# First expert stage: down products from high and low parts, down weights kept in SBUF, up weights of each tile fetched from DRAM

## The reference, cut to what matters

```python
xhat = (x - mu) * rsqrt(var + LN_EPS)
xn = xhat * ln_g[e] + ln_b[e]                      # 256 features
h = relu(xn @ w1[e].T + b1[e])                     # up: 256 -> 1024
y = x + h @ w2[e].T + b2[e]                        # down: 1024 -> 256
out = a * y + (1 - a) * x                          # a = sigmoid(x @ centroids[e])
```

## Time and profile before

| | us |
|---|---|
| median of 3 runs | 1677.14 (1675.1 to 1678.51) |
| profiled execution, device time | 1680.14 |
| its span in the trace | 1678.3 |
| PE busy in the span | 1491.0 (89%) |
| DVE busy | 1002.0 (60%) |
| ACT busy | 882.1 (53%) |
| POOL busy | 833.9 (50%) |
| last step of `routing` 0 on DVE ends | 562.6 |
| up(0) starts on PE | 572.8 |
| finish(31) on DVE ends | 813.2 |

### The profile page before, as it was taken

The page is one execution under the profiler, slowest core; times in us unless marked ns, Lnnn a source line. Parts: engine busy times, 40 slices in busy tenths (PEclk is TensorE's granted clock), DMA queues, the critical chain, the costliest instruction groups (busy, mean ns, idle before and its releaser), DMA issues. The chain is left out here.

```text
span 1678.3 us, 50328 instructions
## 1 busy us (share of the span) xinstructions
PE 1491.0 (89%) x17142; PEld 1239.3 (74%) x17143; DVE 1002.0 (60%) x2228; ACT 882.1 (53%) x1626; POOL 833.9 (50%) x1145
## 2 busy tenths in 40 slices
PE   6999999999996499999599999999999646999677
PEld 4777777777774499999478888888888524888566
DVE  3677677677663433333247677777777577777544
ACT  3777777777774244443266566656665323333233
POOL 3576676666663111111256666666666305333263
PEclk8999999999996699999799999999999757999889
DMA  5111211110100611111212222221110042333475
GB/s 145 58 53 58 83 59 48 59 34 23 34 18 12 261 35 38 38 34 34 86 33 75 67 92 71 75 90 44 44 48 25 16 141 88 129 130 131 127 232 182
DMA packets 63184, 127.98 MB, mean 76 GB/s; under 512 B 11106, under 2 KB 35870, under 8 KB 59590
## 3 DMA queue, kind: packets, MB, share of 16 engines
q1 hardware_dynamic: 52798, 99.03, 18.2%
q0 software_dynamic: 10320, 28.07, 6.0%
HBM read 94.77 MB, written 32.29 MB: 76 GB/s over the span
## 5 line engine op out<-in xcount | busy, mean ns | idle before, releaser
L1017 DVE TENSOR_REDUCE a_mx<-a_SM 100x2 bf16<-100x722 f32 x384 | 351.4, 915 | 201.1 <-PE a_SM L459 197.8
L737 ACT ACTIVATE a_Pr<-a_ST 120x1600 f32<-120x1600 f32 (+3 forms) x192 | 225.0, 1172 | 125.5 <-PE a_ST L491 123.8
L501 PE MATMUL a_M<-a_Pr,a_V 120*32 120x100 f32 (+3 forms) x4608 | 176.2, 257 | 0.0
L459 PE MATMUL a_SM<-a_KT,a_QM 32*100 32x362 f32 x768 | 152.6, 393 | 25.9 <-DVE a_mx L1017 25.6
L787 POOL TENSOR_TENSOR a_rstd<-a_ve,a_powers 100x1 f32<-100x1 f32 x192 | 118.7, 618 | 96.2 <-DVE a_ve L986 94.5
L501 PEld LDWEIGHTS a_M<-a_Pr,a_V 120*32 120x32 f32 (+3 forms) x4608 | 135.8, 120 | 21.7 <-issue 12.8
L862 POOL TENSOR_TENSOR a_cl<-a_ct,a_ch 128x724 fp32r<-128x724 f32 x62 | 107.3, 1731 | 42.9 <-DVE a_o L1059 42.9
L386 PE MATMUL a_M<-a_wvh,a_ch 128*120 128x256 f32 (+1 forms) x384 | 123.8, 322 | 3.1 <-ACT a_KF L623 3.1
L852 POOL TENSOR_TENSOR a_KL<-a_KF,a_KT 128x724 fp32r<-128x724 f32 x64 | 111.5, 1742 | 26.7 <-ACT a_KT L631 15.4
L1534 PEld LDWEIGHTS e_PH<-e_xT,e_wS 128*128 128x128 f32 x1024 | 120.9, 194 | 4.2 <-issue 2.7
L1534 PE MATMUL e_PH<-e_xT,e_wS 128*128 128x128 f32 x1024 | 121.4, 277 | 2.1 <-DVE e_xT L1612 2.1
(11 more groups left out here) (219 smaller groups left out, 3872.3 us busy)
## 6 DMA issues: line engine op xcount, KB each, us to landing
w<-in_E_w SPq DMA_DIRECT2D x24, 1024.0 KB, 7.1
a_ct<-in_ctx SPq DMA_DIRECT2D x64, 362.0 KB, 3.2
gated_rows<-g_hs SPq DMA_DIRECT2D x57, 256.0 KB
keep_rows<-a_keep SPq DMA_DIRECT2D x64, 100.0 KB
tile_rows<-e_y SPq DMA_DIRECT2D x32, 128.0 KB, 1.7
X<-in_E_b SPq DMA_DIRECT2D x1, 4096.0 KB
x_rows<-X SPq DMA_DIRECT2D x32, 100.0 KB
g_xr<-x_rows SPq DMA_DIRECT2D x25, 128.0 KB
```

What stands on the lines that cost most here:

```text
L459: last = nc.tensor.matmul(SM[0:LQ, half, 0:LKP], QM[b.p][rows, chunk, m, :], KT[b.p][rows, chunk, :], start=True, stop=True)
L501: last = nc.tensor.matmul(M0[VW * j:VW * (j + 1), g * LQ:(g + 1) * LQ], V[b.p][0:n, kt, h, :], Pr[0:n, kt, POS[h] * LQ:(POS[h] + 1) * LQ], ...
L737: nc.scalar.activation(Pr[0:n, s, :].rearrange("p (r q) -> p r q", r=GROUPS), ST[0:n, :, 0:PER * LQ], ACT.Exp, scale=SCALE).then_inc(exp_d ...
L1017: V_.tensor_reduce(pair, SM[0:LQ, :, 0:LK], AX_X, ALU.max).then_inc(max_done, 1)
```

## The change

1. The buffer `w1`, which attention 0 fills, now gets the down weights of the first expert layer. The second buffer and its 8 MB of transfers in `routing` 0 are gone.
2. The up weights of each tile come straight from DRAM into `wS`: SP reads the tile's expert and starts a transfer of 1 MB (`up_weights`). It waits for `h_ps` as ACT's copy did. ACT's copy is gone. SP's order is up_weights(j+3), store(j).
3. The down product is made from parts: a value is split into a high part, rounded to fp32r, and a low part, the rest. Per tile ACT makes the high part of `hT` (128x1024) and of the tile's down weights (128x2048); DVE subtracts for the low part of the weights (128x2048) and of the second half of `hT` (128x512); POOL subtracts for the first half of `hT` (128x512). PE does 24 fp32r products (high by high, high by low, low by high) in place of 8 fp32 products, and waits for all three low parts.
4. DVE's order becomes columns(j+2), hidden(j+1), hidden_low(j+1), down_low(j+1), finish(j).
5. `xs` has two buffers, `gather` starts two tiles ahead and takes its row numbers straight from `toks`, without the copy. POOL's stream is written out for all 32 tiles and holds gather(j+2), hidden_low(j).

```diff
@@ expert_tiles: buffers @@
-        w1 = env["w1"]
+        w2 = env["w1"][:].rearrange("p e c f -> p e (c f)")
         ident = env["kept"]["ident"]
-        w2 = env["second_buf"]
         lng, lnb, b1, b2 = (dst for dst, _ in env["small"])
         small_loaded, SMALL = env["small_loaded"], 16 * len(env["small"])
-        gidx = sb("gidx", [128, 1], I32)
-        xs = sb("xs", [128, D])
+        xs = [sb(f"xs{p}", [128, D]) for p in range(2)]
         xT = sb("xT", [128, DC, 128])
-        hT = [sb(f"hT{p}", [128, G, 128]) for p in range(2)]
+        hT_at = [(nc.sbuf_base + 31) // 32 * 32]
+        hT = [sb("hT0", [128, G, 128])]
+        hT_at.append((nc.sbuf_base + 31) // 32 * 32)
+        hT.append(sb("hT1", [128, G, 128]))
+        hT_low = [nc.alloc_sbuf_tensor_at(f"{tag}hT_low{p}", [128, G, 128], F32R, offset=hT_at[p]) for p in range(2)]
+        hT_high = [sb(f"hT_high{p}", [128, G, 128], F32R) for p in range(2)]
+        w2_high = [sb(f"w2_high{p}", [128, G, D], F32R) for p in range(2)]
+        w2_low = [sb(f"w2_low{p}", [128, G, D], F32R) for p in range(2)]
         wS = [sb(f"wS{p}", [128, DC, F]) for p in range(2)]
         y = [sb(f"y{p}", [128, D]) for p in range(2)]
...
         @block.sync
         def _(sp):
-            def store(j, p, r):
+            def up_weights(j, p, first):
+                e = expert_of(sp, j)
+                if not first:
+                    sp.wait_ge(h_ps, j * 2 - 2)
+                sp.dma_start(wS[p][:].rearrange("p c f -> p (c f)"),
+                             t["w1"][:, bass.ds(e, 1)].rearrange("p o c f -> p (o c f)")).then_inc(w_staged[p], 16)
+            def store(j, p):
                 sp.wait_ge(y_ready, j + 1)
                 sp.dma_start(t["ys"][bass.ds(j * 128, 128), :], y[p][:]).then_inc(y_stored[p], 16)
-            with sp.Fori(0, NT // 2) as i:
+            up_weights(0, 0, True)
+            up_weights(1, 1, True)
+            up_weights(2, 0, False)
+            with sp.Fori(0, NT // 2 - 2) as i:
                 for p in range(2):
-                    store(i * 2 + p, p, i)
-            if NT % 2:
-                store(NT - 1, 0, NT // 2)
-            sp.wait_ge(y_stored[0], 16 * ((NT + 1) // 2))
-            sp.wait_ge(y_stored[1], 16 * (NT // 2))
+                    up_weights(i * 2 + (p + 3), 1 - p, False)
+                    store(i * 2 + p, p)
+            for j in range(NT // 2 * 2 - 4, NT):
+                if j + 3 < NT:
+                    up_weights(j + 3, (j + 3) % 2, False)
+                store(j, j % 2)
+            for p in range(2):
+                sp.wait_ge(y_stored[p], 16 * (NT // 2))
         @block.gpsimd
         def _(pool):
-            def gather(j, first):
-                if not first:
-                    pool.wait_ge(x_ps, j)
-                pool.sem_inc(turns, 1)
-                nc.gpsimd.tensor_copy(gidx[:], env["toks"][:, bass.ds(j, 1)]).then_inc(idx_ready, 1)
-                pool.wait_ge(idx_ready, j + 1)
-                pool.sem_inc(turns, 1)
-                nc.gpsimd.indirect_dma_start(xs[:], None, t["keep"], bass.IndirectOffsetOnAxis(gidx[:], 0)
-                                             ).then_inc(rows_loaded, 16)
-            gather(0, True)
-            with pool.Fori(1, NT) as j:
-                gather(j, False)
-        def expert_of(engine, j):
-            return engine.value_load(env["tile_e"][0:1, bass.ds(j, 1)], min_val=0, max_val=E - 1)
+            def gather(j):
+                if j >= 2:
+                    pool.wait_ge(x_ps, j - 1)
+                nc.gpsimd.indirect_dma_start(xs[j % 2][:], None, t["keep"],
+                                             bass.IndirectOffsetOnAxis(env["toks"][:, j:j + 1], 0)
+                                             ).then_inc(rows_loaded[j % 2], 16)
+            def hidden_low(j):
+                p = j % 2
+                pool.wait_ge(h_high, j + 1)
+                nc.gpsimd.tensor_tensor(hT_low[p][:, 0:HALF].rearrange("p g q -> p (g q)"),
+                                        hT[p][:, 0:HALF].rearrange("p g q -> p (g q)"),
+                                        hT_high[p][:, 0:HALF].rearrange("p g q -> p (g q)"), ALU.subtract
+                                        ).then_inc(h_low_pool, 1)
+            gather(0)
+            gather(1)
+            for j in range(NT):
+                if j + 2 < NT:
+                    gather(j + 2)
+                hidden_low(j)
         @block.tensor
         def _(pe):
-            def rows(j, first):
-                pe.wait_ge(rows_loaded, j * 16 + 16)
+            def rows(j, p, r, first):
+                pe.wait_ge(rows_loaded[p], r * 16 + 16)
                 if not first:
                     pe.wait_ge(xT_ready, j)
                 for c in range(DC):
-                    last = nc.tensor.transpose(PX[:, c * 128:(c + 1) * 128], xs[:, c * 128:(c + 1) * 128], ident[:])
+                    last = nc.tensor.transpose(PX[:, c * 128:(c + 1) * 128], xs[p][:, c * 128:(c + 1) * 128], ident[:])
                 last.then_inc(x_ps, 1)
...
             def down(j, p, far):
-                e = expert_of(pe, j)
-                pe.wait_ge(hT_act, j + 1)
-                pe.wait_ge(hT_dve, j + 1)
+                pe.wait_ge(h_low_dve, j + 1)
+                pe.wait_ge(h_low_pool, j + 1)
+                pe.wait_ge(w2_low_ready, j + 1)
                 if far >= 2:
                     pe.wait_ge(y_ready, j - 1)
-                for g in range(G):
-                    rhs = w2[:, bass.ds(e, 1), g, :].rearrange("p o f -> p (o f)")
-                    last = nc.tensor.matmul(PY[:, p, 0:D], hT[p][:, g, :], rhs, start=(g == 0), stop=(g == G - 1))
+                steps = [(g, h, w) for g in range(G) for h, w in ((hT_high, w2_high), (hT_high, w2_low), (hT_low, w2_high))]
+                for k, (g, h, w) in enumerate(steps):
+                    last = nc.tensor.matmul(PY[:, p, 0:D], h[p][:, g, :], w[p][:, g, :],
+                                            start=(k == 0), stop=(k == len(steps) - 1))
                 last.then_inc(y_ps, 1)
...
+            def hidden_high(j, p):
+                act.wait_ge(hT_act, j + 1)
+                act.wait_ge(hT_dve, j + 1)
+                nc.scalar.activation(hT_high[p][:].rearrange("p g q -> p (g q)"),
+                                     hT[p][:].rearrange("p g q -> p (g q)"), ACT.Copy).then_inc(h_high, 1)
+            def down_high(j, p, far):
                 e = expert_of(act, j)
-                if not first:
-                    act.wait_ge(h_ps, j * 2 - 2)
-                nc.scalar.activation(wS[p][:], w1[:, bass.ds(e, 1)].rearrange("p o c f -> p (o c) f"), ACT.Copy
-                                     ).then_inc(w_staged, 1)
-            stage(0, 0, True)
-            stage(1, 1, True)
+                if far >= 2:
+                    act.wait_ge(y_ps, j - 1)
+                nc.scalar.activation(w2_high[p][:].rearrange("p g d -> p (g d)"),
+                                     w2[:, bass.ds(e, 1)].rearrange("p o f -> p (o f)"), ACT.Copy
+                                     ).then_inc(w2_high_ready, 1)
+            down_high(0, 0, 0)
+            down_high(1, 1, 1)
             act.wait_ge(small_loaded, SMALL)
             for j in range(2):
                 hidden(j, j, j)
-                stage(j + 2, j, False)
+                hidden_high(j, j)
+            down_high(2, 0, 2)
             with act.Fori(1, NT // 2 - 1) as i:
                 for p in range(2):
                     hidden(i * 2 + p, p, 2)
-                    stage(i * 2 + (p + 2), p, False)
+                    hidden_high(i * 2 + p, p)
+                    down_high(i * 2 + (p + 1), 1 - p, 2)
...
+            def hidden_low(j, p):
+                dve.wait_ge(h_high, j + 1)
+                V_.tensor_tensor(hT_low[p][:, HALF:G].rearrange("p g q -> p (g q)"),
+                                 hT[p][:, HALF:G].rearrange("p g q -> p (g q)"),
+                                 hT_high[p][:, HALF:G].rearrange("p g q -> p (g q)"), ALU.subtract
+                                 ).then_inc(h_low_dve, 1)
+            def down_low(j, p):
+                e = expert_of(dve, j)
+                dve.wait_ge(w2_high_ready, j + 1)
+                V_.tensor_tensor(w2_low[p][:].rearrange("p g d -> p (g d)"),
+                                 w2[:, bass.ds(e, 1)].rearrange("p o f -> p (o f)"),
+                                 w2_high[p][:].rearrange("p g d -> p (g d)"), ALU.subtract).then_inc(w2_low_ready, 1)
...
             with dve.Fori(1, (NT - 2) // 2) as i:
                 for p in range(2):
-                    j = i * 2 + p
-                    hidden(j, p, 2)
-                    columns(j + 2, False)
-                    finish(j, p, i, 2)
-            for j in range(NT - 2, NT):
-                hidden(j, j % 2, 2)
-                if j + 2 < NT:
-                    columns(j + 2, False)
-                finish(j, j % 2, j // 2, 2)
+                    columns(i * 2 + (p + 2), False)
```

(64 more changed lines are left out.)

20 lines of the change are left out of this document (9 added, 11 removed).

## The result

The changed kernel takes 1683.91 us (median of 10 runs, the lowest 1680.53), the kernel before 1677.14 (10 runs, 1673.57 to 1680.52): ratio 1.0038, 95% interval 1.0025 to 1.0051, so 6.8 us slower. Forecast were 1688.2 us and +11.1. Executions in a slow state (one of these ten of the changed kernel, 2679.79 us, and three of 2069 to 2744 us among those of the kernel before in the second group of experiments, e5 to e8) are left out of every ratio and interval, and the two medians given here are the same without it. The profiled execution of the changed kernel took 1680.73 us with a span of 1678.7, almost what the profiled one of before took: within the spans the rest of the program happened to be some 5 us shorter in the one execution than in the other. So I read the stage by itself.

What follows compares the result with a forecast made beforehand. PE bounds the tile loop before; after the change DVE's queue, with its ACT trip and POOL's turns, would. +14.0 (period) - 3.5 (start) + 0.6 (end) = +11.1 us on 1677.14 gives 1688.2 us, range 1679 to 1699.

Steps and rivals of the forecast that it cites:

- the turns: DVE and POOL subtractions reading SBUF alternate by whole instructions, so down_low, ready at 4.5 us, starts at 5.2.
- its faster product pays nothing: PE's down product: 2.89 us instead of 3.46, but PE needs 6.68 a tile and idles 1.07.
- The period: DVE's tile loop: 7.75 us against 7.25, ends 7.45 and 8.1, +14.0 us over 28 tiles; forecast's chance 0.68.
- columns to hidden: DVE, start of columns(j+2) to start of hidden(j+1): 1.1 us, bounds 0.93 and 1.34.
- hidden to hidden_low: DVE's hidden 1.13 us, ACT's rounding 1.05, two semaphore hops of 0.1 each; hidden_low at 3.5 us.
- hidden_low to the true start of down_low: DVE from 3.5 to 5.2 us, the turn with POOL included; bounds of down_low's start 4.5 and 5.5.
- from there to the next columns: DVE: down_low 2.21 us, then 0.35 until the next columns.
- The start: Stage opening until columns(3): -3.5 us, bounds -1.6 and -4.2; up(0) at 569.7, waiting for its weights.
- The end: From columns(31) to the end of finish(31): 19.1 us against 18.5, so +0.6; bounds -1 and +1.
- both rivals: Tile loop: late weights, 1731 us at L = 14; clock halved, 1677 + 77 = 1754; chance 0.09 with other waits.
- The rival in which the turns cost nothing: DVE and POOL share SBUF: down_low at 4.5, period 7.06, -9.3 us, 1667.8; chance 0.10.
- The rival in which PE is the limit: DVE's waits overlap more, PE sets 6.68 us a tile: -20 us, 1657; chance 0.03.

Runs made afterwards that it cites:

- e5: Changed kernel with down_low before hidden_low on DVE, and DVE making all 1024 low columns of hT, POOL none: 1658.40 us, ratio 0.9887 to the kernel before.
- e8: As e5, plus expert's number read before columns and SP waiting for gather(0) before its second 1 MB transfer: 1657.69 us, ratio 0.9885 to the kernel before.
- e1: Changed kernel, but POOL fills its half of hT_low with zeros instead of subtracting: 1668.95 us, ratio 0.9962 to the kernel before.
- e3: Changed kernel with down_low ahead of hidden_low on DVE, all work kept: 1660.47 us, ratio 0.9913 to the kernel before.
- e6: Changed kernel with the expert's number for hidden read before columns and its wait in DVE's loop: 1676.79 us, ratio 0.9996 to the kernel before.
- e2: Changed kernel, but DVE makes the low part of all 1024 columns of hT and POOL none: 1670.65 us, ratio 0.9963 to the kernel before.
- e7: Kernel before with only the up weights' 1 MB transfer by SP replacing ACT's copy; fp32 down and preload stay: 1682.91 us, ratio 1.0025.

## Why the prediction was right, and what was off

**Direction, and the turns: shown.** The chain over hidden, ACT's rounding, POOL's turn and down_low took the place of PE's work alone as the limit. e1 takes the turn's 0.93 us away, e3 the wait for ACT, and with both gone PE is the limit at 6.66 (e5).

**The loop was not the one that I had summed.** I had closed it on DVE within one tile and let PE idle in its shadow. DVE's queue by itself gives 7.17 us, the short tile and every tile of e6; the 7.45 come from the way over two tiles through PE, with the read behind columns' wait (1.85 us from rows to hidden). So "its faster product pays nothing" does not follow in the changed kernel: down is a part of the first piece.

**The period, 7.75 forecast, 7.45 measured: the term columns to hidden was mis-sized.** By steps (forecast; long tile, short tile):
- columns to hidden: 1.1; 1.19, 0.64. Wrong in the mean by 0.18. I had read 0.93 to 1.34 from code in which DVE had been waiting before. With down_low of 3.22 us running, the number for the second tile of the body was read while DVE was still at work, since rows lay 1.21 us ahead of columns there and 0.66 in the long tile. The earlier trace rows has 0.61 of `issue` and the earlier trace rows 0.20; the cover that makes it zero was not in rows of before, and my lower bound of 0.93 missed it. e6 shows that the read is what the 0.47 was.
- hidden to hidden_low: 2.4; 2.31, 2.30. ACT's 1024 columns are recorded at 1.06, forecast 1.05, so the hops cost about 0.1 less than I had put in.
- hidden_low to the true start of down_low: 1.7; 1.70 and 1.70. Right, with POOL's end minus 0.13, the very handing over that the earlier trace rows had shown.
- from there to the next columns: 2.56; 2.53, 2.53. Right.

That makes 7.73 and 7.17; -0.30 in the mean, 28 times, is -8.3 of the sum. The chance given to a period of 7.2 to 7.45 was 0.10; it came out at that edge, within the range given for the forecast's own case. It was in part luck that the total came nearer than the period: the stage's +5.0 us is +5.7 - 0.8 + 0.1, and of the 8.3 us that the period had too much, the start gave 2.7 back.

**The start, -3.5 forecast, -0.8 measured: mis-sized too, and outside its bounds of -1.6 and -4.2.** Counted from the stage's opening columns(3) came 0.8 us earlier, and up(0) 1.5. The weights were not what it waited for; the last packet of the first transfer is in at about 569.1, 4.5 us after its issue, where I had taken 5.5. But rows(0) could start on gather(0)'s rows only at 569.74, 4.1 us after its instruction, not near 567: I had not counted that the gather moves behind the first 1 MB. Then up(0), starting earlier in the slow stretch of the clock (0.50 over 563 to 577), took 6.61 us in place of 5.53. In before and in all the others it lies between 5.16 and 6.64 (e2 and e6), and no run isolates why.

**The end, +0.6 forecast, +0.1 measured.** columns(31) to hidden(31) was a short tile, 7.17 in place of 7.8; down(31), 6.5 later, and at the slow clock, was as forecast (813.44 to 817.94, 4.5 us).

**PE:** down at 2.97 us (645.83 - 642.86) with 0.12 a product, forecast 2.89. Idle 0.26 and 0.83 before down, not 1.07 in each tile. No wait for the weights in the loop, no fall of the clock: both rivals out, with the DMA near the forecast of 170 GB/s. The rival in which the turns cost nothing is out: down_low reads 3.22 us beside POOL's subtraction, and once the turn is really gone (e1) the period is 7.04 and not 7.45. That 7.06 was forecast for it is a coincidence: it had been summed as DVE's queue of one tile, and the 7.04 are the mean of a 6.4 and a 7.7 us tile. The rival in which PE is the limit needed another order of DVE's queue: e5 shows it.

**The rule of the Trainium skill** ("SBUF — State Buffer", SBUF: two separate sides), an exclusive lock for a whole instruction against a GpSimd operation that reads SBUF, was the one that carried the result, and the experiments agree with it: down_low takes 3.22 us while POOL's subtraction, which reads SBUF, runs, and 2.29 without it. Against an operation that only writes, there is POOL's memset in e1, which ran beside the two-input hidden_low with neither held up (0.52 and 0.69 us).

**Open:** what from rows to hidden differs between the two tiles of DVE's body where columns starts equally late behind rows: 1.74 and 2.01 us in e5. The branch back of the loop lies between them, but no kernel without it was run. And the 5 us by which the rest of the program differs between the profiled executions.

## What to carry to other kernels

Work handed to GpSimd that reads SBUF was no help here to a VectorE whose instructions have two SBUF inputs: add both up as one queue before you split. In a queue in order, put the long piece that depends on nothing in the gap of the piece that waits for another engine; here that swap alone was worth 22 us against the changed kernel, more than the 16 us (28 x 0.57) that the faster product can bring. And before a period is summed, follow the waits of one queue into the other engines and back, over more than one tile, and look for each register read at which semaphore wait stands ahead of it: moved ahead of that wait, the read was worth 7.5 us here.

## What the runs showed of the hardware beyond that

- In these rows a gather's instruction on POOL is held up by DVE's subtraction as well if it comes second: started at 648.36, 0.28 us after down_low really began, it lasts 2.83 us and ends 0.83 after it; started 0.05 before down_low (e1) it takes 0.95, and down_low its 2.29 none the less.
- The first gather of 128 rows lands 3.9 to 4.3 us after its instruction in the kernels with the new start, where its packets follow the first 1 MB load, and 5.0 to 5.1 in e7 and before, beside the preload.
- Reading one number from SBUF into a register (0.30 us for the load itself) puts between nothing and 0.65 us of idle time ahead of DVE's hidden in the changed kernels, by what runs ahead of it and by the wait that it stands behind.
- 183 GB/s of transfers into SBUF left a saturated PE as it was: 7.26 us a tile against 7.25.
